# Neural-operator tower on one core: batch statistics taken in the mix, inverse and next forward transform in one stage

## Chip, core and metric

One Trainium2 chip, one core, all in fp32. The metric is the device time of one execution in microseconds (us); the kernel before has a median of 4404.04 us over three runs.

## What is computed

The part that matters is a Fourier neural operator tower of four layers over 64 images of 64x64 pixels with 64 channels:

```python
h = x @ fc0_w + fc0_b                                  # 3 -> 64 channels
for l in range(4):
    xf = rfft2(h)                                      # 32 x 16 modes are kept (16 low, 16 high rows; 16 columns)
    sc = irfft2(einsum('bixy,ioxy->boxy', xf[modes], w[l]))    # complex weights for each mode
    y = sc + einsum('bihw,oi->bohw', h, pw_w[l]) + pw_b[l]     # spectral part + pointwise part
    y = (y - mean(y)) * rsqrt(var(y) + eps) * gamma + beta     # over batch and pixels, for each channel
    h = gelu(y)
out = gelu(h @ fc1_w + fc1_b) @ fc2_w + fc2_b          # head
```

Behind it comes a tail (attention and two mixtures of experts on 64 tokens of 64 numbers for each image), which the change leaves as it is but for the places of two buffers.

## The kernel before

Data lies in pairs: a tile of 128 partitions holds two images of 64 channels (2 MB for a pair, `NP` = 32 pairs, `NG` = 8 groups of `Q` = 4 pairs). All five engines run programs written out by hand, with semaphores; each stage ends in `phase_end`, where every engine waits for the others. SP (SyncE) issues most DMAs in the order of its program, and a wait in it holds back all that follow.

- **Spectrum 0** computes the modes of the input directly from the three-channel x and stores them to `spec_in` (four stores of 4 MB, `sync_spectrum0`).
- **Mix** (`tensor_mix`) goes over 8 slabs `c` of 64 modes. A slab's weights (2 MB) and spectra (2 MB) are loaded, `rotate` on ScalarE and VectorE makes the second copy of the spectra for complex products, TensorE does 64x64 products for each mode on four tiles at once (L444, half slab v in banks 4v to 4v+3), VectorE turns the result (L480), SP stores it to `spec_out`.
- **Inverse** goes over pairs: `rows` (L579) is the inverse transform over rows, four VectorE transposes (L695) turn its result, then for each of four chunks T of 2x512 pixels `spectral` (L602) and `pointwise` (L593) add into the same PSUM banks, ScalarE copies them out with the bias (L659), VectorE takes bn_stats (L703), and ScalarE's queue stores y to `y_dram`. In layers 1 to 3 the pointwise part needs h, so the y of the layer before is loaded and passed through gelu again (L651). At the end come the statistics: `scale` and `shift`.
- **Forward** goes over pairs: load y, gelu (L843), four pixel turns (L848), `w_dft` (L803), two turns (L853), `h_dft` (L820), two turns (L862), store to `spec_in`.
- **Head**: load y, gelu (L947), `first` (L919) into three pairs of banks, gelu (L954), `second` (L930) which gathers one output row for each step.

The order of stages is spectrum 0, mix 0, inverse 0, then (forward, mix, inverse) for layers 1 to 3, the head, the tail.

Of the kernel before, what the change touches and what calls it, by code (L numbers as in the profile page):

```python
# [13 lines left out]
P = 128  # L14
# [13 lines left out]
ENGINES = 5  # L28


def dft_constants():
# [36 lines left out]
    dc[0, 0] = dc[0, K1] = 1  # L68
    consts = {"c_fw_q": fw_q, "c_gh_q": gh_q, "c_ga": np.tile(ga, (2, 1)), "c_fb2": fb2, "c_g0": g0.reshape(P, 4 * K1),
              "c_f0": f0p.reshape(97, 4, P), "c_dc": dc, "c_ident": np.eye(P),  # L70
              "c_half": np.kron(np.full((2, 2), 0.5), np.eye(C))}
    return {k: np.ascontiguousarray(v, dtype=np.float32) for k, v in consts.items()}


def tower_layout(x, fc0_w, fc0_b, w1r, w1i, w2r, w2i, pw_w):
# [12 lines left out]
    out["w_modes"] = np.stack([r, i], 2).reshape(L, NCH, P, MC, C)  # L88
    out["pw_t"] = np.ascontiguousarray(pw_w.transpose(0, 2, 1))
# [13 lines left out]
def build(nc, d, B, out):  # L103
# [5 lines left out]
    with ExitStack() as ctx:  # L109
# [8 lines left out]
        y_dram = nc.dram_tensor("y_dram", [NP, P, PX], F32, kind="Internal").ap()  # L118

# [7 lines left out]
        pw = sb("pw", [P, P])  # L127
        wst = sb("wst", [P, C])
        pwb = sb("pwb", [P, 1])
        gamma = sb("gamma", [P, 1])  # L130
# [6 lines left out]
        stats = sb("stats", [P, NP * 48])  # L137
# [4 lines left out]
        ARENA = 45800  # L142
# [36 lines left out]
        const_loaded, basis_loaded, cols_loaded = sem("const_loaded"), sem("basis_loaded"), sem("cols_loaded")  # L179
        X0_LOADS = [(0, 1), (1, 2), (2, 4), (4, 6), (6, 8)]  # L180
        x0_loaded = [sem(f"x0_loaded{i}") for i in range(len(X0_LOADS))]
        x0_load_of = [j for j, (a, b) in enumerate(X0_LOADS) for i in range(a, b)]
# [4 lines left out]
        pw0_done, pw0_copied = sem("pw0_done"), sem("pw0_copied")  # L187
# [12 lines left out]
        spec0 = [at(S0 + t * NCH * MB * MC, NCH, MB, 2, K1) for t in range(3)]  # L200
        ROUND_AT = {(i, h): (i - 3) * 2 + h for i in range(3, NQ + 1) for h in range(2)}
# [3 lines left out]
        def sync_spectrum0(sp):  # L205
            sp.dma_start(g0, d["c_g0"]).then_inc(basis_loaded, 16)
            for j, (a, b) in enumerate(X0_LOADS):
                sp.dma_start(x0_all[:, 4 * a:4 * b], d["x_rows"][4 * a:4 * b].rearrange("q p x -> p q x")).then_inc(x0_loaded[j], 16)
            for c in range(2):
                load_weights(sp, 0, c)  # L210
# [7 lines left out]
        def tensor_spectrum0(pe):  # L218

            def rows0(i):  # L220
                pe.wait_ge(x0_loaded[x0_load_of[i]], 16)
# [36 lines left out]
            pe.wait_ge(basis_loaded, 16)  # L258
# [18 lines left out]
            pe.matmul(bank[1][:, 0:1], pw[:], fc0b[:], start=True, stop=True).then_inc(pw0_done, 1)  # L277

        def vector_spectrum0(dve):
# [30 lines left out]
            dve.wait_ge(pw0_done, 1)  # L310
            for u in range(2):
                half_p = slice(u * C, (u + 1) * C)
                dve.tensor_copy(wst[half_p, :], bank[0][half_p, u * C:(u + 1) * C]).then_inc(pw0_copied, 1)
# [56 lines left out]
        def third(l, c):  # L370

            return l * (USES[c % 3] * 16) + (c // 3 * 16 + 16)

# [1718 lines left out]
```

## Time and profile before

| | |
|---|---|
| runs | 4381.96, 4404.04, 4449.41 us; median 4404.04 |
| span of the profiled execution | 4441.0 us (its own run time is not listed; the span is 8 us under the slowest run) |
| mean granted TensorE clock | 0.868 |
| PE / PEld / DVE / ACT busy | 74% / 47% / 54% / 47% |
| moved to and from HBM | 708.56 MB read, 405.14 MB written |

PE is TensorE, PEld its weight loads, DVE VectorE, ACT ScalarE, POOL GpSimd, SP SyncE; "SPq" is the queue of DMAs that SP issues. The granted clock is given as a share of 2.4 GHz. Each fp32 matmul of the program appears as two instructions. A busy share is an average over stages with different limits, so what counts is the table by stage, and inside a stage the order of the instructions.

### The profile page before, as it was taken

How to read it: one execution, taken by the hardware profiler on the slowest of the kernel's cores; microseconds unless marked ns; L12 is line 12 of the kernel's file. 1: busy time of each engine (PE TensorE's matmuls, PEld its weight loads, DVE VectorE, ACT ScalarE, POOL GpSimd, SP SyncE). 2: the span in 40 equal slices, each digit the busy share in tenths (PEclk: the TensorE clock that was granted, in tenths of full speed). 3: DMA queues.
4: the chain of work that ended last, by engine and by line, in shares of the span. 5: the costliest groups of instructions: out<-in, count | busy, mean ns of one | idle time of the engine just before them, and what ended most of it. 6: DMA issues, size and time to landing. Idle time of an engine off the chain costs nothing. (4 is left out here: it accounts for less than half of the span.)

```text
span 4441.0 us, 122046 instructions
## 1 busy us (share of the span) xinstructions
PE 3288.5 (74%) x54724; PEld 2081.7 (47%) x54724; DVE 2394.9 (54%) x3232; ACT 2086.9 (47%) x1724; POOL 28.9 (1%) x48
## 2 busy tenths in 40 slices
PE   6878866666888565596886556768877998559777
PEld 4756644455555343473554334745542222543432
DVE  3466668753666587544665777346651000554556
ACT  2133354421666644214665543236667998222321
POOL 0000000000000000000000000000000000100000
PEclk8989988888999888898998778989998999669688
DMA  8978887678999867598999676889996542003053
GB/s 305 351 192 241 238 265 271 256 288 336 345 391 380 295 249 264 228 327 330 381 377 333 248 264 249 321 294 399 391 340 231 190 173 99 10 10 68 1 97 67
DMA packets 181646, 1120.67 MB, mean 252 GB/s; under 512 B 25497, under 2 KB 31841, under 8 KB 107262
## 3 DMA queue, kind: packets, MB, share of 16 engines
q1 hardware_dynamic: 140924, 843.27, 52.7%
q10 hardware_dynamic: 39234, 269.45, 17.5%
q8 instruction: 379, 6.21, 0.5%
q0 software_dynamic: 1024, 1.05, 0.1%
q14 instruction: 85, 0.70, 0.0%
HBM read 708.56 MB, written 405.14 MB: 251 GB/s over the span
## 5 line engine op out<-in xcount | busy, mean ns | idle before, releaser
L602 PEld LDWEIGHTS bank<-fb,arena 64*64 64x64 f32 x16384 | 671.9, 199 | 512.9 <-issue 498.8
L602 PE MATMUL bank<-fb,arena 64*64 64x128 f32 x16384 | 677.9, 293 | 236.8 <-ACT arena L659 183.2
L659 ACT ACTIVATE arena<-bank,pwb 128x1024 f32<-128x1024 f32 x512 | 558.7, 1111 | 472.5 <-PE bank L593 337.0
L703 DVE BATCH_NORM_STATS2 stats<-arena 128x6 f32<-128x512 f32 x1024 | 627.8, 676 | 176.4 <-ACT arena L659 175.9
L843 ACT ACTIVATE arena<-arena,shift,scale 128x1024 f32<-128x1024 f32 x384 | 443.5, 1229 | 438.4 <-DMA arena<-y_dram 437.9
L593 PE MATMUL bank<-arena,wst 64*64 64x512 f32 x4096 | 629.9, 633 | 11.0 <-issue 10.9
L695 DVE STREAM_TRANSPOSE arena<-bank 128x512 f32<-128x512 f32 x512 | 321.1, 685 | 501.5 <-PE bank L579 501.5
L803 PE MATMUL bank<-arena,fwq 32*32 32x512 f32 x6144 | 322.6, 824 | 362.4 <-DVE arena L848 319.3
L651 ACT ACTIVATE arena<-arena,shift,scale 128x2048 f32<-128x2048 f32 x192 | 401.4, 2092 | 353.4 <-issue 206.2
L444 PE MATMUL bank<-arena 64*64 64x128 f32 x8192 | 455.4, 393 | 108.0 <-ACT arena L459 89.0
L444 PEld LDWEIGHTS bank<-arena 64*64 64x64 f32 x8192 | 395.0, 153 | 168.1 <-issue 118.8
L848 DVE STREAM_TRANSPOSE arena<-arena 128x1024 f32<-128x1024 f32 x384 | 440.1, 1203 | 16.2 <-ACT arena L843 16.2
L820 PE MATMUL bank<-arena,ghq 32*32 32x256 f32 x12288 | 366.0, 429 | 49.6 <-issue 45.1
L579 PE MATMUL bank<-arena,ga 64*64 64x512 f32 x2048 | 307.7, 619 | 127.8 <-DMA arena<-spec_out 108.5
L820 PEld LDWEIGHTS bank<-arena,ghq 32*32 32x32 f32 x12288 | 281.7, 111 | 140.5 <-issue 109.1
L803 PEld LDWEIGHTS bank<-arena,fwq 32*32 32x32 f32 x6144 | 101.0, 117 | 496.6 <-issue 486.0
L459 ACT ACTIVATE arena<-arena 64x4096 f32<-64x4096 f32 x32 | 115.9, 3621 | 448.2 <-DMA arena<-spec_in 448.2
L480 DVE STREAM_TRANSPOSE arena<-bank 128x512 f32<-128x512 f32 x256 | 159.5, 683 | 253.3 <-PE bank L444 134.8
L919 PE MATMUL bank<-arena,fc 64*128 64x512 f32 x1024 | 265.3, 626 | 17.9 <-ACT arena L947 16.5
L954 ACT ACTIVATE arena<-bank,fc1b 128x1024 f32<-128x1024 f32 x256 | 267.8, 1122 | 14.3 <-PE bank L919 14.3
L853 DVE STREAM_TRANSPOSE arena<-bank 128x1024 f32<-128x1024 f32 x192 | 227.2, 1221 | 84.9 <-PE bank L803 84.4
L579 PEld LDWEIGHTS bank<-arena,ga 64*64 64x64 f32 x2048 | 115.4, 138 | 249.9 <-issue 236.5
(195 smaller groups left out, 2364.4 us busy)
## 6 DMA issues: line engine op xcount, KB each, us to landing
arena<-y_dram SPq DMA_DIRECT2D x224, 2048.0 KB, 10.2
y_dram<-arena ACTq DMA_DIRECT2D x256, 1024.0 KB, 13.2
arena<-in_w_modes SPq DMA_DIRECT2D x32, 2048.0 KB, 17.2
arena<-spec_in SPq DMA_DIRECT2D x32, 2048.0 KB, 14.7
spec_out<-arena SPq DMA_DIRECT2D x128, 512.0 KB, 15.6
arena<-spec_out SPq DMA_DIRECT2D x112, 512.0 KB, 16.9
spec_in<-arena SPq DMA_DIRECT2D x24, 2048.0 KB, 13.6
spec_in<-arena SPq DMA_DIRECT2D x4, 4096.0 KB, 12.0
```

What stands on the lines that cost most here:

```text
L444: mm = pe.matmul(bank[4 * v + q][ROW[half], k * 2 * B:(k + 1) * 2 * B], w_sb[u][ROW[row], mode, :], s_sb[u][ROW[row], :, :, mode], start=( ...
L579: mm = pe.matmul(bank[2 * v + r][CHAN[par], :], ga[k_p, r * S:(r + 1) * S], grp[p // Q % 2][k_p, :, par * Q + q, :], start=True, stop=True ...
L593: mm = pe.matmul(bank[4 + T % 2 * 2 + i][CHAN[v], :], wst[CHAN[i], :], hin[p % 3][CHAN[i], px:px + BK], start=False, stop=True, tile_posit ...
L602: mm = pe.matmul(hpx(bank[4 + T % 2 * 2 + i][CHAN[v], :])[:, :, j * S:(j + 1) * S], a2[p % 2][CHAN[i], v, :, 4 * T + j], hpx(fb2[CHAN[i], :]),
L651: act.activation(x, x, ACT.Gelu, bias=shift[:], scale=scale[:]).then_inc(h_ready, 1)
L659: act.activation(hpx(yout[u])[:, :, T * BK:(T + 1) * BK], banks[:, 4 + T % 2 * 2:6 + T % 2 * 2, :], ACT.Identity, bias=pwb[:]).then_inc(y_ ...
L695: dve.transpose(a2[p % 2][:, :, v * HB + c0:v * HB + c0 + 16, :].rearrange("p v c r -> p c v r"), banks[:, 2 * v:2 * v + 2, :].rearrange(" ...
L703: dve.bn_stats(stats[:, p * 48 + 6 * t:p * 48 + 6 * t + 6], hpx(yout[p % 2])[:, i, T * BK:(T + 1) * BK]).then_inc(y_seen, 1)
L803: mm = pe.matmul(bank[g][QUAD[c], :], fwq[QUAD[g], s * 32:(s + 1) * 32], hT[q % 2][QUAD[g], s, :, c * CQ:(c + 1) * CQ], start=(s == 0), st ...
L820: mm = pe.matmul(bank[4 + c][QUAD[j], 0:256], ghq[QUAD[c], col:col + K1], t1[q % 2][QUAD[c], v:4:2, hh, :, ri * M2:(ri + 1) * M2], start=( ...
L843: act.activation(x, x, ACT.Gelu, bias=shift[:], scale=scale[:]).then_inc(f_ready, 1)
L848: dve.transpose(hT[p % 2][:, :, 16 * v:16 * v + 16, :].rearrange("p s h c -> p h s c"), hf[p % Q][:, v * 2 * BK:(v + 1) * 2 * BK].rearrang ...
```

## The change

1. The mean and variance of y are computed in the mix from its spectra (Parseval) and from the pointwise product, before the inverse. For this the mix gets, for each half slab, a `product` on TensorE (pointwise weights times the spectra), a ScalarE copy of it, two ScalarE squares with a sum, two VectorE cross products with a sum. The sums of squares of the pointwise part come from the stage before.
2. Since scale and shift are known ahead, one stage (`*_fuse`) does inverse, gelu, the next layer's pointwise product and the forward transform for each pair. What goes to `y_dram` is the next pointwise product p, and VectorE adds it to the spectral part one layer later.
3. The last inverse and the head are one stage (`*_last`).
4. For modes of column 0 the weights are made symmetric: GpSimd does that (`gpsimd_even`), for layer 0 in spectrum 0, for the others in fused stage 0. For layer 0 the sum of squares of the pointwise part comes from a Gram matrix of x.

The stages are now spectrum 0, mix 0, fused 0, (mix, fused) for layers 1 and 2, mix 3, last, tail. The core of the diff:

```diff
 def sync_spectrum0(sp):
...
+            load_modes(sp, 0, 0)
+            load_weights(sp, 0, 1)
+            sp.wait_ge(even_stored, 64)
+            load_even(sp, 0)
             for t in range(NB):
                 sp.wait_ge(fc0_first, 4 * t + 4)
...
+        def tensor_mix(pe, l):
+            def product(n):
+                c, v = n // 2, n % 2
...
+                if n > 1:
+                    pe.wait_ge(mixed_turned, (l * NU + n - 1) * 2)
...
+            def spectra(n):
...
+                pe.wait_ge(prod_copied, l * NU + n + 1)
...
+            product(0)
+            for n in range(NU):
+                spectra(n)
+                if n + 1 < NU:
+                    product(n + 1)
...
+            def copy_product(n):
+                v = n % 2
+                act.wait_ge(prod_done, l * NU + n + 1)
+                act.activation(x2[v], banks[:, 4 * v:4 * v + 4, :].rearrange("p q x -> p (q x)"), ACT.Copy, scale=2.0).then_inc(prod_copied, 1)
...
+        ROWS_SLOT = (0, 1)
+        Y_SLOT = (0, 0, 1, 0)
+        NEXT_SLOT = (0, 1, 1, 1)
...
+            # TensorE, y_of(p, T)
+                if T == 2 and p > 0:
+                    pe.wait_ge(squared, n * 4)
+                if T == 3:
+                    pe.wait_ge(squared, n * 4 + 1)
...
+            # TensorE, iteration n
+                if now:
+                    y_of(n, 0)
+                if before:
+                    next_of(n - 1, 2)
+                if now:
+                    y_of(n, 1)
+                if before:
+                    next_of(n - 1, 3)
+                if after:
+                    rows_of(n + 1, 0)
+                if before:
+                    w_dft(n - 1, 0)
+                if now:
+                    y_of(n, 2)
+                    next_of(n, 0)
+                if after:
+                    rows_of(n + 1, 1)
+                if before:
+                    w_dft(n - 1, 1)
+                if now:
+                    y_of(n, 3)
+                    next_of(n, 1)
+                if before:
+                    h_dft(n - 1)
...
+            def evict(p, T):
+                n = l * NP + p
+                act.wait_ge(px_turned, n * 4 + T + 1)
+                act.wait_ge(next_done, n * 4 + T + 1)
+                act.sem_inc(waited[act.engine], 1)
+                act.activation(chunk(p, T), slot(NEXT_SLOT[T]), ACT.Copy).then_inc(evicted, 1)
+                act.activation(slot(NEXT_SLOT[T]), slot(NEXT_SLOT[T]), ACT.Square, accum_out=acc[:, p * 4 + T:p * 4 + T + 1]).then_inc(squared, 1)
```

(The two comment lines in the diff name the engine; they are not in the code.) The order of the other two engines in iteration n of a fused stage: VectorE `add(n,0)`, `px_turn(n-1,2)`, `h_turn(n-2)`, `add(n,1)`, `px_turn(n-1,3)`, `turn_rows(n+1,0)`, `add(n,2)`, `w_turn(n-1,0)`, `px_turn(n,0)`, `turn_rows(n+1,1)`, `add(n,3)`, `w_turn(n-1,1)`, `px_turn(n,1)`; ScalarE `evict(n-1,1)`, `gelu(n,0)`, `evict(n-1,2)`, `gelu(n,1)`, `evict(n-1,3)`, `gelu(n,2)`, `evict(n,0)`, `gelu(n,3)`. Fused stage 0 has no adds; there `y_of` also multiplies x by its weights `wx`, and gelu reads PSUM. In `rows` the output of a matmul goes to PSUM in the order "p (c r k) -> p r k c", where it was in one piece before. In the last stage `rows` and y use slot 0 (banks 0 and 1) alone, and `first` has two slots where it had three.

## Rows read from the trace of the kernel before

**Rows 1.** Busy time by stage: window, length, busy us of each engine, clock, DMA
```profile
0.00:83.00 83.00, 51.44 (x324) 34.89 (x324) 32.71 (x35) 17.55 (x17) 0.59 (x7) 0.93 0.82 304
229.00:619.00 390.00, 314.82 (x5636) 236.96 (x5636) 251.02 (x403) 143.09 (x131) 0.00 (x0) 0.92 0.84 231
619.00:943.00 324.00, 198.60 (x6144) 128.48 (x6144) 259.59 (x256) 149.07 (x129) 0.00 (x0) 0.83 0.71 267
943.00:1097.00 154.00, 112.97 (x2048) 97.23 (x2048) 58.11 (x72) 29.08 (x9) 0.00 (x0) 0.85 0.87 327
1097.00:1521.00 424.00, 329.58 (x5636) 219.63 (x5636) 245.91 (x400) 268.12 (x195) 0.00 (x0) 0.89 0.94 354
2943.00:3362.00 419.00, 322.44 (x5636) 214.32 (x5636) 245.19 (x400) 268.00 (x194) 0.00 (x0) 0.91 0.93 358
3362.00:3774.00 412.00, 386.23 (x2048) 107.86 (x2048) 6.28 (x10) 389.25 (x321) 15.53 (x32) 0.98 0.46 165
```

**Rows 2.** Timeline of mix 1, TensorE's matmuls and VectorE's turns: start, us
```profile
954.85 55.54 PE L444 MATMUL bank<-arena 64*64 64x128 f32 x1012 [20.59 <-ACT arena L459]
...
962.16 2.51 DVE L480 STREAM_TRANSPOSE arena<-bank 128x512 f32<-128x512 f32 x4 [3.98 <-PE bank L444]
969.16 2.51 DVE L480 STREAM_TRANSPOSE arena<-bank 128x512 f32<-128x512 f32 x4 [4.49 <-PE bank L444]
```

**Rows 3.** Timeline of SP's queue, last stores of mix 1
```profile
1074.72 1.74 SPq L391 DMA_DIRECT2D spec_out<-arena  x4
```

**Rows 4.** Timeline of inverse 0 at full clock
```profile
239.38 2.44 DVE L695 STREAM_TRANSPOSE arena<-bank 128x512 f32<-128x512 f32 x4
...
241.96 1.99 PE L579 MATMUL bank<-arena,ga 64*64 64x512 f32 x8 [8.65 <-DVE arena L695]
...
245.95 1.10 PE L602 MATMUL bank<-fb,arena 64*64 64x128 f32 x32
...
246.86 1.04 PE L593 MATMUL bank<-arena,wst 64*64 64x512 f32 x8
...
247.72 1.04 PE L579 MATMUL bank<-arena,ga 64*64 64x512 f32 x8
...
247.97 1.11 ACT L659 ACTIVATE arena<-bank,pwb 128x1024 f32<-128x1024 f32 x1 [0.22 <-PE bank L593]
```

**Rows 5.** Timeline of the last `h_dft` of forward 0
```profile
931.51 2.75 PE L820 MATMUL bank<-arena,ghq 32*32 32x256 f32 x128 [1.50 <-DVE arena L862]
934.29 1.31 DVE L862 STREAM_TRANSPOSE arena<-bank 128x512 f32<-128x512 f32 x2 [2.93 <-PE bank L820]
```

**Rows 6.** Groups by line and shape: count, busy us, mean ns, idle before
```profile
L843 ACT ACTIVATE arena<-arena,shift,scale 128x1024 f32<-128x1024 f32 x384 | 443.5, 1229 | 438.4 <-DMA arena<-y_dram 437.9
L345 ACT ACTIVATE arena<-bank 128x1024 f32<-128x1024 f32 x16 | 16.3, 1023 | 31.4 <-PE bank L252 31.3
L680 ACT ACT_TABLE_LOAD x4 | 5.1, 1283 | 59.5 <-DMA y_dram<-arena 59.5
...
L848 DVE STREAM_TRANSPOSE arena<-arena 128x1024 f32<-128x1024 f32 x384 | 440.1, 1203 | 16.2 <-ACT arena L843 16.2
L1383 DVE TENSOR_TENSOR arena<-bank,arena 128x512 f32<-128x512 f32 x16 | 10.3, 688 | 11.0 <-PE bank L1247 11.0
```

**Rows 7.** Timeline of the head, TensorE alone
```profile
3606.90 1.99 PE L919 MATMUL bank<-arena,fc 64*128 64x512 f32 x8
3608.81 1.07 PE L930 MATMUL bank<-arena 128*32 128x512 f32 x8
3609.81 1.99 PE L919 MATMUL bank<-arena,fc 64*128 64x512 f32 x8
```

**Rows 8.** Spectrum 0's stores, small loads, GpSimd arithmetic: timeline, DMA, group
```profile
37.77 29.84 SPq L214 DMA_DIRECT2D spec_in<-arena  x4
...
arena<-spec_out SPq DMA_DIRECT2D x4, 256.0 KB, 3.2
...
L1570 POOL TENSOR_SCALAR arena<-arena 128x384 f32<-128x384 f32 x1 | 1.2, 1246 | 4.9 <-POOLq L171 4.9
```

More of the change, by code:

```diff
@@ L452, in scalar_mix @@
[L452 to L459 removed]
+                sp.wait_ge(mixed_stored[u], l * (NCH * 32) + NCH * 32)
+                sp.sem_inc(waited[sp.engine], 1)
@@ new lines, in turn @@
+            def turn(n):
+                c, v = n // 2, n % 2
+                if v == 0 and c > 1:
+                    dve.wait_ge(mixed_stored[c % 2], l * (NCH * 32) + (c // 2 * 64))
+                    dve.sem_inc(waited[dve.engine], 1)
+                modes = banks[:, 4 * v:4 * v + 4, :].rearrange("p q (k r b) -> p b r (q k)", k=4, r=2)
+                for j in range(2):
+                    dve.transpose(m_sb[c % 2][:, 4 * j:4 * j + 4, v, :], modes[:, 32 * j:32 * j + 32]).then_inc(mixed_turned, 1)
@@ new lines, in vector_mix @@
+            rotate(0)
+            for n in range(NU):
+                cross(n)
+                turn(n)
+                if n % 2 == 0 and n // 2 + 1 < NCH:
+                    rotate(n // 2 + 1)
+            base = l * BN_STEPS
+            dve.wait_ge(layer_loaded, l * 96 + 96)
+            dve.wait_ge(crossed, (l * NU + NU) * 2)
+            dve.sem_inc(waited[dve.engine], 1)
+            dve.tensor_tensor(acc_p[:], acc[:], acc_w[:], ALU.mult).then_inc(bn_step, 1)
+            dve.scalar_tensor_tensor(out=bn[:, 9:10], in0=dc[:, 1:2], scalar=0.5, in1=dc[:, 0:1], op0=ALU.mult, op1=ALU.add).then_inc(bn_step, 1)
@@ L845, in vector_forward @@
[L845 to L854 removed]
+            rows_of(0, 0)
@@ new lines, in tensor_fuse @@
+            rows_of(0, 1)
+            for n in range(NP + 1):
+                now, before, after = n < NP, n > 0, n + 1 < NP
+                if now:
[22 more added lines that the diff above has]
+                    h_dft(n - 1)
@@ L884, in build, with gpsimd_fuse @@
+        def gpsimd_fuse(pool, l, first):
+            pool.wait_ge(pw_loaded, l * 32 + 32)
+            pool.sem_inc(waited[pool.engine], 1)
+            gpsimd_negate(pool, l + 1)
+            if first:
+                pool.wait_ge(negated, 2)
+                for k in range(1, L):
+                    gpsimd_even(pool, k)
+                pool.wait_ge(even_stored, 16 * N_EVEN * L)
+        fc1_done, fc1_gelu, fc2_used = sem("fc1_done"), sem("fc1_gelu"), sem("fc2_used")
         fc2_ready, tok_ready = sem("fc2_ready"), sem("tok_ready")
@@ L909, in tensor_head @@
[L909 to L919 removed]
+        FC_SLOT = (2, 1)
```

1195 lines of the change are left out of this document (704 added, 491 removed).

## Prediction

> **What bounds the kernel now.** I read the table by stage first [rows 1]: its windows are cut where the first DMA of each stage is issued. The thirteen stages of the tower take 3774 us, the tail the other 667, which the change leaves alone. From 619 to 3362 run three identical layers (forward, mix, inverse), 2743 us or 914 each. The three kinds have different limits. An inverse stage of a later layer moves 354 GB/s with its DMA engines 94% busy: each pair is read and written (4 MB), and TensorE, at 329 of 424 us, is not far behind. A forward stage is short of everything: it waits for its loads, and its clock falls to 0.83. A mix stage has TensorE busy without a break once it has begun: 1012 matmuls stand in one row of 55.54 us, and VectorE's turns come each 7.00 us (962.16, 969.16) for a half slab of 128 instructions, so 54.9 ns each [rows 2]. The head is ScalarE's: 389 of 412 us [rows 1]. So bytes matter in the inverse stages (390, 424 and 419 us in the rows), and engine time or engine order in the rest.
>
> **What the change removes.** Five passes of 67 MB over `y_dram`: three reads of forward, the last inverse's write, the head's read. It removes bn_stats, and the statistics at the end of each inverse. What is late next is the question: in the fused stage each pair moves 4.5 to 5 MB, under 14 us at 354 GB/s, and I find below that the engines need far more than that. So the bytes are worth only what they held up.
>
> **Mix.** Each half slab now has a `product` on TensorE, ahead of it a wait for nothing new, and behind it a ScalarE copy (`prod_copied`) for which the next `spectra` on TensorE waits. So the product and the copy stand on TensorE's path. The product's moving operand has `b` innermost, 64 floats apart, as `spectra` has. In L444 a 128-column instruction on one of four tiles took 54.9x4 = 220 ns [rows 2]; 512 contiguous columns (L593, 8 instructions on 4 tiles in 0.86 us, 246.86 to 247.72) took 430 ns, half as much per column [rows 4]. The product gives each tile 2048 pass-columns: 3.5 us at the first rate, 1.7 at the second; I take 3.5, since its stride is that of L444. ScalarE's two squares (1024 elements, about 1.1 each by L345 [rows 6]) lie beside the product; then the copy of 2048 elements, 1.9 us (twice L345's 1.02 less one start). With 0.25 us from TensorE to ScalarE (247.72 to 247.97 [rows 4]) and 0.15 back to TensorE (VectorE's end 241.82 to 241.96 [rows 4]), a half slab takes 7.0+3.5+0.25+1.9+0.15 = 12.8 us against 7.0. VectorE's cross products, turns and rotation (6 us a half slab) and the slab's 6.3 MB in 25.7 us stay under it. The stage: 12 us to the first operand as now, 5.8 for the first product and copy, 15x12.8+7.0 = 199, 6 for the last squares, cross and turns, 22 from the last store to the next stage as now (1074.72 to 1097 [rows 1, 3]), 2 for slips: 247 against 154. Mix 0 the same +93 on its 146: 239. The bound from below is a product at 1.7 us: 11.7 a half slab, -72 us over four stages; from above, one more slow stretch of clock, +40.
>
> **Spectrum 0.** Stores of spectra now stand in SP's queue behind `wait_ge(even_stored, 64)` and `load_even`. Today they are issued from 37.77 to 67.6 and the stage ends at 83 [rows 8]. GpSimd must first do four chunks, one after another: two loads, two tensor_scalar and one tensor_tensor of 512 elements, one store. At L1570's 1.25 us for 384 elements the arithmetic is some 5 us, and a load and a store of 256 KB, at 3.2 us to landing plus their issue and waits, some 8 [rows 8]: 13 a chunk, begun at about 33 when x is in: 85. Then 16.8 MB at 350 GB/s: 48 us, 132 in all. The Gram matmuls hide in that, and the negated weights, for which the first product waits, are GpSimd's last step there. The same chunks for layers 1 to 3 (12x13 = 156 us) lie in fused stage 0, where SP asks for them only at pair 30. Bounds 90 and 150.
>
> **Fused stages, layers 1 and 2.** Engine work of one pair: VectorE 2 row turns, 4 adds, 4 pixel turns, 2 W turns at 1.2 us (L848; L1383's 0.69 for 512 elements gives the same for the add) and 1.3 of H turns: 15.7. TensorE 4 groups of y and 4 of next at 0.9, 2 of rows at 0.87, W and H DFT at 2.75 (each now 128 instructions; H took 931.51 to 934.29 [rows 5]): 14.5. ScalarE 4 gelus of 1.23 and 4 copies with squares of 2.15: 13.5 [rows 4 to 6]. No engine is near 20, but the order is written out, and banks are few: `next` and y share slots. I walk one pair from `add(n,0)` = 0. px_turn 2, h_turn, add 1, px_turn 3 end at 6.1. `evict(n-1,3)` must wait for that turn, 2.15 us; y_of(n,2) waits for its square, 0.15+0.9+0.25: add(n,2) starts at 9.65. Add, W turn, pixel turn 0 end at 13.2; evict(n,0) and y_of(n,3) again 3.5: add(n,3) at 16.7. Add and W turn end at 19.05; h_dft (0.15+2.75) must precede y_of(n+1,0) on TensorE (0.9+0.25): the next add at 23.1. That is 63% of TensorE, the share of forward, whose clock was 0.83; the gaps here are 2 to 3 us and not 7, inverse has 0.89 [rows 1]. At half clock the same walk gives some 31.5. With 0.86 in between, 24.8. A stage: 32x24.8, 6 to fill, 12 for the last pair's DFTs and 12 for its spectra to land: 824, against 914-154 = 760 now. Bounds 22 (full clock, copies at L345's 1.02 with overlap) and 26.5 a pair. SP now issues the stores too, and load(n+2) stands behind store(n-1), but two pairs ahead: over 40 us for one landing, so nothing.
>
> **Fused stage 0.** No adds; y carries L593's product (1.76 a group), and gelu reads PSUM. The same walk: gelu 0 ends at 1.2, evict 2 at 3.4, gelu 1 at 4.6, evict 3 at 6.8, y2 and gelu 2 at 10.2, evict 0 at 12.35, y3 14.3, next 1 at 15.1, h_dft 17.9, y0 19.9. TensorE is 90% busy, so 21 with the clock: 32x21+30 = 702. Now 390+324 = 714. Bounds 18.9 and 23.
>
> **Last stage.** TensorE a pair: 8 x 0.96 (`first`, 1.91 for two), 4 x 1.0 (`second`) [rows 7], 5.2 for rows and y: 16.9. ScalarE 4x1.23+8x1.05 = 13.3. Slot 0's six turns of 2.5 us are covered by them, but `first` waits for the gelu of two before, behind gelu(n,3): one stall of 1.1 us: 18.3. 32x18.3+25 = 611, against 419+412 = 831. Bounds 17.0 and 20.
>
> **Sum.** 132+239+702+247+824+247+824+247+611+667 = 4740 against the span of 4441: +299. That span lies 8 us below the slowest of the three runs, 0.8% above their median; the difference is carried over: 4404+299 = 4703.
>
> **Rivals.** (A) The waits that I walked are covered, and the busiest engine sets the pair: 16.3 us in fused 1 and 2 (VectorE) and 17.9 in fused 0 (TensorE): 552+552+603 in place of 824+824+702, -643, so 4060. For it: each engine has idle time. Against it: evict(n-1,3), evict(n,0) and h_dft each stand between two uses of a bank pair that the code names. It decides where the mean fused pair falls under 20.4 us, 3.1 below my 23.5: there the kernel is no slower than before. (B) `rows` now writes PSUM with 32 floats between columns; if that costs as the stride of L444 does, 0.9 becomes 1.75 for each half. The last stage takes all of it, +56, fused 0 about +28, fused 1 and 2 +13 each: 4813. No row shows a strided PSUM write. (C) Product, squares and copy vanish under something in the mix, which stays at 154: 4331. Against: TensorE's unbroken row. (D) Each Square between gelus reloads ScalarE's table, 1.28 us twice (the load of L680 [rows 6]): 8x1.28x96 pairs = 983 us more on a path that has no room: about 5690. Against: gelu and Identity alternate without one.
>
> The Trainium skill bears on two of these. Its page "SBUF — State Buffer", in "Door 1: The DMA port swizzle", has lines of 16 bytes in SBUF and 8 in PSUM, and says "any non-contiguous PSUM access pattern significantly slows down matmuls". Of SBUF the trace agrees (220 against 107 ns for 128 columns); of PSUM this rule is rival B, and nothing here shows it; the time by it is B's. The Trainium skill's page "ScalarE: Activation LUTs", in "Table sets: the hidden batching unit", has cheap functions such as copy and identity in every set, but does not list square beside gelu there: that is rival D.
>
> **Chances.** My forecast 0.63, A 0.12, B 0.15, C 0.07, D 0.03. The bounds, taken together and not all at one end, put my own case within 4500 to 4880. Two per cent, about what a measurement of this kernel can tell from no change, is 4316 to 4492. Faster: 0.12, all of A. Same: C and the low end of mine, 0.13. Slower: 0.75. The range 4370 to 4900 leaves out A, D, half of C and the tails.
>
> **What would show it.** VectorE's turns in mix 12.8 us apart and ScalarE's 2048-element copy ahead of each restart of TensorE; a fused pair (distance of H turns) of 23 to 25 us with VectorE about 65% busy, adds of chunk 2 and 3 waiting for matmuls that wait for a square; a first-stage end near 132 set by GpSimd; the last stage near 610 with TensorE over 90%. I am wrong if a fused pair is under 20.4 us, or the mix is under 200.

## The result and the profile after

The changed kernel takes 5179.12 us (median of four runs, 5155.51 to 5191.25) against 4415.83 on the same chip: a ratio of 1.176, 95% interval 1.169 to 1.184. It is slower, as forecast, but by 763 us where the forecast had 299. The profiled execution spans 5169.4 us at a mean clock of 0.85.

Busy time by stage of the changed kernel, with the columns of [rows 1] (window, length, busy us of PE, PEld, DVE, ACT, POOL, clock, DMA share, GB/s). The windows are spectrum 0, mix 0, fused 0, fused 1, fused 2, last:

```profile
0.00:124.20 124.20, 68.61 (x460) 50.34 (x460) 34.03 (x42) 17.58 (x17) 25.30 (x37) 0.82 0.63 230
124.20:357.80 233.60, 171.76 (x2434) 127.30 (x2434) 96.79 (x119) 97.60 (x93) 0.00 (x0) 0.80 0.61 208
357.80:1217.40 859.60, 684.66 (x15360) 368.38 (x15360) 346.36 (x320) 405.18 (x513) 71.42 (x73) 0.93 0.53 139
...
1451.90:2431.00 979.10, 652.18 (x14336) 369.08 (x14336) 488.25 (x448) 422.40 (x513) 0.37 (x1) 0.81 0.59 174
...
2666.10:3614.80 948.70, 646.38 (x14336) 366.33 (x14336) 488.46 (x448) 422.47 (x513) 0.37 (x1) 0.83 0.61 179
...
3848.40:4505.90 657.50, 606.67 (x7168) 266.20 (x7168) 242.44 (x202) 418.70 (x385) 63.40 (x128) 0.97 0.35 127
```

Beside the forecast's terms:

| stage | forecast | measured | difference |
|---|---|---|---|
| spectrum 0 | 132 | 124.2 | -8 |
| four mixes | 239+3x247 = 980 | 233.6+234.5+235.1+233.6 = 937 | -43 |
| fused 0, 1, 2 | 702+824+824 = 2350 | 859.6+979.1+948.7 = 2787 | +437 |
| last | 611 | 657.5 | +47 |
| tail | 667 | 663.5 | -4 |
| span | 4740 | 5169.4 | +429 |

So the miss lies in the fused stages (the other terms, -8, -43, +47 and -4, cancel by luck), and the question of the experiments is what stands there. Against the kernel before, by stage: the mixes take 329 us more, spectrum 0 41 more, and fused and last stages together 3445 us where inverse, forward and head took 3083 [rows 1, with the four mixes at 146 + 3x154], 362 more; the forecast had them 122 less. A half slab of the mix, which answers to [rows 2], in the timeline (start, us):

```profile
1296.98 1.88 ACT L631 ACTIVATE arena<-bank 128x2048 f32<-128x2048 f32 x1 [0.87 <-PE bank L581]
...
1299.00 7.17 PE L603 MATMUL bank<-arena 64*64 64x128 f32 x128 [2.09 <-ACT arena L631]
...
1308.59 1.06 PE L581 MATMUL bank<-arena,wneg 64*64 64x256 f32 x4
...
1309.70 1.88 ACT L631 ACTIVATE arena<-bank 128x2048 f32<-128x2048 f32 x1 [0.73 <-PE bank L581]
...
1311.72 7.25 PE L603 MATMUL bank<-arena 64*64 64x128 f32 x128 [2.07 <-ACT arena L631]
```

From one start of L603 to the next is 12.72 us: 6.98 of spectra, 3.67 of product, 0.05 to the copy, the copy's 1.88, 0.14 back. That is the sum of the prediction (12.8), where 3.5 for the product and 0.25 to the copy erred in opposite directions.

A stretch of fused 1, TensorE alone, then SyncE's queue in the same stretch:

```profile
1838.81 1.68 PE L799 MATMUL bank<-arena,ga 64*64 64x256 f32 x16
1840.41 1.49 PE L947 MATMUL bank<-arena,fwq 32*32 32x256 f32 x64
1841.84 1.17 PE L809 MATMUL bank<-fb,arena 64*64 64x128 f32 x26
1845.51 0.49 PE L809 MATMUL bank<-fb,arena 64*64 64x128 f32 x5 [2.50 <-issue]
...
1851.92 1.19 PE L809 MATMUL bank<-fb,arena 64*64 64x128 f32 x30 [0.63 <-ACT bank L1014]
1858.24 0.58 PE L809 MATMUL bank<-fb,arena 64*64 64x128 f32 x2 [5.13 <-issue]
1858.56 1.99 PE L933 MATMUL bank<-arena,wst 64*64 64x512 f32 x8
1861.39 4.55 PE L964 MATMUL bank<-arena,ghq 32*32 32x256 f32 x128 [0.84 <-DVE arena L1053]
...
1840.31 1.63 SPq L840 DMA_DIRECT2D y_dram<-arena  x2
1842.05 2.58 SPq L779 DMA_DIRECT2D arena<-y_dram  x1
```

This is the thing to see. A group of y is 32 instructions without a wait in it, but TensorE stops after 26 of them for 2.50 us, and in another group after 30 for 5.13 us, and the releaser is "issue": nothing that the profile shows. The H transform that follows (1861.39) stands in a stretch of granted clock 0.5 and takes 4.55 us against 2.75 in [rows 5]. The DMA view of 1836 to 1868, share of the DMA engines in tenths and GB/s in slices of 0.8 us:

```profile
DMA  0799999997899989989988999979731000000000
GB/s 0 300 384 387 384 394 379 374 348 154 184 266 225 174 266 266 225 174 215 328 246 287 328 328 348 430 312 369 287 141 51 8 0 20 0 0 0 20 0 0
```

By the records of single packets, 2 MB go to `spec_in` in packets of 2 KB up to 1842.4, at 374 to 394 GB/s; then the two stores to `y_dram` in packets of 8 KB, which start up to 1851.9, with the DMA engines as busy but at 154 to 266 GB/s for the most part; then the load, in packets of 16 KB, most of them started by 1858. Queue 8 carries TensorE's instructions; the page has it as:

```profile
q8 instruction: 517, 8.47, 0.7%
```

517 packets of 16 KB. TensorE has 64,580 matmuls, as many weight loads and 2848 other records, 132,008 in all: 255 a packet, so 256 slots of 64 bytes. e1 and e6 below have 119,720 and 119,653 records and 469 packets, again 255. The kernel before has 379 packets for 112,504 records: 297 a packet. Its inverse stages have 250 to 260 a packet, but its forward stages, which run as a loop on TensorE (`pe.Fori(1, NG)`, seven rounds), 390 to 594, with no packet started for up to 107 us. The fused stages have no such loop inside: the 29,424 records of fused 1 are 116 packets. So the change also put straight code in the place of looped code.

**Where TensorE stalls.** I numbered TensorE's records from the first of each stage and took every pause over 0.5 us between two weight loads with no semaphore wait between them. In fused 1 there are 108; 52 of them, 137.5 us, fall on numbers whose remainder by 256 is 76, 77 or 78. The two above are numbers 11,852 and 12,109. In fused 2 it is the same remainder, 47 pauses and 121.8 us; in fused 0, 182 to 184, 47 pauses and 116.8 us. The rest are spread over all remainders, 69 us in fused 0 and 87 to 90 in the other two, there mostly the 2.1 us ahead of L933 once a pair, a wait that the walk contains. The second piece of evidence is the time at which queue 8's packets start. One started at 1843.10 and one at 1855.88, with 12.8 us between them, and TensorE went on at 1845.51 and 1858.24: 2.4 us after each. Of the 146 pauses of the three stages 136 are like that: work resumes 2.1 to 2.6 us after a block's packet starts. Of the 196 other pauses 15 are. So these are waits for the next block of instructions, and the block is late because its packet starts late, among some 20 us of bulk packets. Together 376 us. In the last stage, which stores nothing to `y_dram`, the same count gives 6 us. In the kernel before it gives 46 us in inverse 0 and 8 to 15 in the later ones (a looped forward stage can't be numbered like that).

### The profile page after: what moved, and what is told of

Its sections match the earlier page's. It is cut to its first block and busy times, and to the rows that moved or that the text cites. A ratio compares the mean times of both kernels' runs of the same rounds, so it can differ in the third digit from the quotient of the medians.

```text
span 5169.4 us, 141776 instructions
## 1 busy us (share of the span) xinstructions
PE 3833.6 (74%) x64580; PEld 2200.9 (43%) x64580; DVE 2339.6 (45%) x2458; ACT 2245.7 (43%) x2564; POOL 173.6 (3%) x249
## 5 line engine op out<-in xcount | busy, mean ns | idle before, releaser
L826 DVE TENSOR_TENSOR arena<-bank,arena 128x1024 f32<-128x1024 f32 x384 | 468.2, 1219 | 1047.0 <-PE bank L809 1047.0
L809 PEld LDWEIGHTS bank<-fb,arena 64*64 64x64 f32 x16384 | 570.4, 197 | 639.9 <-issue 584.3
L1006 ACT ACTIVATE arena<-arena,shift,scale 128x1024 f32<-128x1024 f32 x256 | 317.7, 1241 | 862.0 <-DVE arena L826 853.7
L933 PE MATMUL bank<-arena,wst 64*64 64x512 f32 x3072 | 496.0, 687 | 146.8 <-issue 146.8
L603 PE MATMUL bank<-arena 64*64 64x128 f32 x8192 | 461.6, 393 | 132.5 <-ACT arena L631 100.0
L603 PEld LDWEIGHTS bank<-arena 64*64 64x64 f32 x8192 | 408.2, 173 | 212.8 <-issue 186.8
L1013 ACT ACTIVATE arena<-bank 128x1024 f32<-128x1024 f32 x384 | 392.2, 1021 | 199.2 <-DVE arena L1046 141.8
L799 PE MATMUL bank<-arena,ga 64*64 64x256 f32 x4096 | 321.0, 430 | 126.6 <-DMA arena<-spec_out 54.9
L1014 ACT ACTIVATE bank<-bank 128x1024 f32<-128x1024 f32 x384 | 391.7, 1020 | 0.0
L947 PE MATMUL bank<-arena,fwq 32*32 32x256 f32 x12288 | 321.7, 412 | 57.1 <-issue 45.7
L684 DVE SCALAR_TENSOR_TENSOR arena<-bank,arena 128x1024 f32<-128x1024 f32 x128 | 156.3, 1225 | 411.6 <-ACT arena L642 410.9
L1003 ACT ACTIVATE arena<-bank,shift,scale 128x1024 f32<-128x1024 f32 x128 | 154.2, 1205 | 410.2 <-PE bank L913 410.2
L575 PE MATMUL bank<-arena,wst 64*64 64x512 f32 x512 | 232.8, 1033 | 84.8 <-ACT arena L626 84.8
L642 ACT ACTIVATE arena<-bank 128x1024 f32<-128x1024 f32 x128 | 131.2, 1025 | 363.6 <-PE bank L603 355.7
## 6 DMA issues: line engine op xcount, KB each, us to landing
spec_in<-arena SPq DMA_DIRECT2D x4, 4096.0 KB, 24.8
```

The costliest lines, as they stand in the source:

```text
L603: mm = pe.matmul(bank[4 * v + q][ROW[h], k * 2 * B:(k + 1) * 2 * B], w_sb[c % 3][ROW[row], mode, :], z[ROW[row], :, :, mode], start=(swap ...
L799: mm = pe.matmul(bank[2 * s + v][CHAN[par], :].rearrange("p (c r k) -> p r k c", c=16, r=2)[:, r], ga[k_p, r * S:(r + 1) * S], grp[p // Q ...
L809: mm = pe.matmul(hpx(bank[2 * s + i][CHAN[v], :])[:, :, j * S:(j + 1) * S], a2[p % 2][CHAN[i], :, v, 4 * T + j], hpx(fb2[CHAN[i], :]), sta ...
L826: dve.tensor_tensor(chunk(p, T), slot(s), chunk(p, T), ALU.add).then_inc(y_added, 1)
L933: mm = pe.matmul(bank[2 * NEXT_SLOT[T] + v][CHAN[i], :], wst[CHAN[v], :], pb[p % NS][CHAN[v], i, T * BK:(T + 1) * BK], start=True, stop=Tr ...
L947: mm = pe.matmul(bank[4 + g][QUAD[c], 0:256], fwq[QUAD[g], s * 32:(s + 1) * 32], hT[p % 2][QUAD[g], i, :, s, c * CQ:(c + 1) * CQ], start=( ...
```

## Experiments

Each run is compared with the kernel before on its chip; the intervals are +-0.004 to 0.008. Its medians beside the runs were 4416 to 4435 us, so a difference in us between two rows can be off by some 20; the ratios and the stages of the traces are not. "Stalls" are the pauses at a block's border, counted as above, in fused 0, 1, 2.

| run | us | ratio | fused 0, 1, 2 | stalls |
|---|---|---|---|---|
| the change | 5179 | 1.176 | 860, 979, 949 | 117, 138, 122 |
| e1 half the W transform | 5071 | 1.146 | 798, 943, 957 | 100, 124, 123 |
| e2 quarter stores and loads | 4795 | 1.084 | 723, 843, 837 | 17, 33, 31 |
| e3 H transform later | 5006 | 1.133 | 840, 885, 889 | 101, 150, 158 |
| e4 copy in halves | 5064 | 1.144 | 858, 974, 962; mixes 205 to 213 | 114, 128, 124 |
| e5 = e3 + e4 | 4899 | 1.110 | 835, 885, 888 | 91, 127, 136 |
| e6 W transform in one piece | 5106 | 1.155 | 809, 961, 960 | 82, 77, 81 |
| e7 quarter loads | 5135 | 1.161 | 857, 960, 958 | 113, 119, 122 |
| e8 = e5 + e6 | 4823 | 1.092 | 758, 888, 884 | 38, 110, 108 |
| e9 quarter stores | 4943 | 1.114 | 856, 858, 844 | 113, 46, 42 |
| e10 stores on ScalarE's queue | 5226 | 1.176 | 950, 948, 947 | 179, 124, 120 |
| e11 stores in two, each at once | 4897 | 1.104 | 765, 874, 868 | 50, 58, 57 |
| e12 = e8 + e10 | 4903 | 1.104 | 871, 871, 874 | 87, 104, 101 |
| e13 stores in two, together | 4977 | 1.123 | 771, 910, 905 | 56, 87, 87 |
| e14 stores in four | 4885 | 1.102 | 745, 873, 872 | 33, 55, 61 |
| e15 = e8 + e11 | 4648 | 1.047 | 738, 817, 817 | 24, 65, 65 |
| e16 = e8 + e14 | 4644 | 1.046 | 745, 809, 818 | 26, 51, 63 |
| e17 before, stores in two | 4344 | 0.982 | | 2 in inverse 0 |

**TensorE's work.** e1 does the W transform for s = 0 alone, so half of the work is left out. e6 does all of it in one 512-column piece; that piece must also wait for the H turns of the pair before, and the first W turn for the whole piece, so e6 changes the order a little as well.

```diff
-                for s in range(2):
+                for s in range(1):                     # e1
...
-                            mm = pe.matmul(bank[4 + g][QUAD[c], 0:256], ...
-                                           hT[p % 2][QUAD[g], i, :, s, c * CQ:(c + 1) * CQ],
+                            mm = pe.matmul(bank[4 + g][QUAD[c], :], ...      # e6
+                                           hT[p % 2].rearrange("p i h s c -> p (i h) s c")[QUAD[g], :, s, c * CQ:(c + 1) * CQ],
```

> The changed kernel, with half of the W DFT of each pair left out (only s = 0, so the spectra are wrong in value): 64 of a pair's 448 matmul instructions and their weight loads go. In my walk of the pair the W DFT lies beside ScalarE's copy and square, off the chain. Theory S (TensorE's instruction stream is not delivered fast enough: the gaps of 5.5 us a pair in fused 1 in which TensorE waits for nothing): the gaps shrink at least with the number of instructions, 0.8 to 1.6 us a pair, so 75 to 150 us over the 96 fused pairs: 5030 to 5105 us. Theory O (the order of the engines alone, with links longer than I walked): less than 25 us, about 5165.

> The changed kernel with the W DFT of a pair in one piece of 512 columns in place of two of 256, as the kernel before had it: 64 matmul instructions and 64 weight loads fewer for each pair, all work kept. Theory S (supply of instructions): as with half of the W DFT left out, 80 to 110 us less, about 5085; the gaps without a releaser shrink. Theory O: the W DFT was beside ScalarE's copy, so under 25 us. It could be slower if the one piece, which must now wait for the H turns of the pair before, delays y_of(n,2).

Both have half the instructions for the W transform, a seventh fewer in the stage. Fused 0 falls by 62 and 51 us, fused 1 by 36 and 18, and fused 2 rises by 8 and 12. e6's stalls in fused 1 and 2 are 40 to 60 us less, but its clock there is 0.79 where it was 0.81 and 0.83, and TensorE is about as long busy (646 us) with a seventh fewer instructions. Both totals lie near what the theory of supply expected, but the gain sits mostly in fused 0 and the stalls of e1 fell by 29 us alone, so neither run names a cause.

**The order.** e3 puts the H transform of pair n-1 behind `y_of(n + 1, 0)`, off the walk's path.

```diff
                 if now:
                     y_of(n, 0)
+                if n > 1:
+                    h_dft(n - 2)
...
-                if before:
-                    h_dft(n - 1)
```

> The changed kernel with h_dft(n-1) moved on TensorE behind y_of(n+1,0), all work kept. By the walk of the pair the link W turn, h_dft (2.9 us), y_of(n+1,0) goes, and VectorE's own order follows: 2.8 us a pair less in fused 1 and 2, 2.0 in fused 0: -240 us, about 4940. Theory S (the supply of instructions sets the pair more than the order): the gaps grow as TensorE's work gets denser, and half or less of it is seen: 5060 to 5150.

It gives 94 and 60 us in fused 1 and 2, 2.9 and 1.9 a pair: the 2.9 + 0.15 us that the walk has for that step, less a part; in fused 0 it gives 0.6 a pair, of 2.0 expected. In all 5006 us, between the two theories (4940, 5060 to 5150). The stalls of fused 1 and 2 rose to 150 and 158, so the gain is one of order: the walk had it right, and the denser pair gave some 50 us back to the stalls of these two stages.

**The traffic.** e2 stores and loads only the first quarter of each pair's columns at `y_dram`, e7 loads a quarter and stores all, e9 stores a quarter from layer 1 on and loads all.

```diff
-sp.dma_start(y_dram[p].rearrange("(v c) (i x) -> i c v x", v=2, i=2)[i], pb[p % NS][CHAN[i]])
+sp.dma_start(y_dram[p].rearrange("(v c) (i x) -> i c v x", v=2, i=2)[i][:, :, 0:BK], pb[p % NS][CHAN[i]][:, :, 0:BK])
```

> The changed kernel, where only a quarter of each pair goes to y_dram and comes back (the rest of the tile keeps old values, so the result is wrong in value). All instructions and waits of the compute engines are the same. Theory S1 (the instruction blocks are late because bulk transfers share the DMA engines): gaps of TensorE without a releaser halve, 80 us off each of fused 1 and 2 and 40 off fused 0, about 4980. Theory S2 (the delay of a block is its own, whatever the load): no change beyond 25 us. Theory O: no change either, since no load or store was on the chain.

> The changed kernel where only a quarter of each pair is loaded from y_dram, but all of it is stored (values wrong). Loading and storing at a quarter gave 385 us. If the bytes count alike, whatever their direction, about half of it, 4990 us (fused 0, which never loaded pairs, stays as it was, 860). If only the stores count (4 KB runs written by two transfers each), it stays above 5120; if only the loads, it comes near 4800.

> From layer 1 on only a quarter of each pair is stored (leaves the rest of the values in DRAM as layer 0 left them); layer 0 stores whole, and all loads are whole. Theory (the stores hold up TensorE's instruction blocks, the loads don't): fused stages 1 and 2 fall from 979 and 949 to those of the run in which both were a quarter, 843 and 837; fused stage 0 stays at 860; in all 5179 - 136 - 112 = 4930, ratio 1.115. Rival (the two only do harm together): stages 1 and 2 halfway, 900, in all 5050. Rival (the stores are innocent): 5179.

Busy time by stage, fused 0 and fused 1 of e2, then of e9:

```profile
358.54:1081.83 723.29, 635.09 (x15360) 349.71 (x15360) 346.35 (x320) 404.45 (x513) 71.43 (x73) 0.98 0.33 96
1316.52:2159.53 843.01, 586.01 (x14336) 340.67 (x14336) 488.11 (x448) 422.58 (x513) 0.37 (x1) 0.90 0.28 86
```

```profile
357.15:1213.40 856.25, 684.24 (x15360) 366.06 (x15360) 346.33 (x320) 405.52 (x513) 71.41 (x73) 0.92 0.54 140
1447.81:2305.94 858.13, 600.82 (x14336) 346.68 (x14336) 488.11 (x448) 422.41 (x513) 0.37 (x1) 0.89 0.40 140
```

e2 comes near the stages of the prediction: 723, 843, 837 against 702, 824, 824, all engine work kept. That is 384 us, nearly twice the 200 that I expected of it. TensorE's busy time falls by 66 us as well, since its clock rises from 0.81 to 0.90. e9 shows that the stores do it: fused 0, whose stores are whole, stays at 856; fused 1 and 2 fall by 121 and 105 and their stalls from 138 and 122 to 46 and 42. e7's loads change these two stages by -19 and +9. In fused 1 and 2 e7 and e9 move the same 2.5 MB of `y_dram` a pair, so it is not the sum of the bytes. Nor is it the time that packets take of the DMA engines: their share in fused 1 is 0.48 of 960 us in e7, 461 us, less than in e13 below (0.58 of 910), and e7 has the more stalls, 119 us against 87. What e7 keeps, and e2, e9, e11, e13 and e14 don't, are the 8 KB packets of the stores.

**The queue.** In e10 ScalarE issues the stores, behind `gelu(n, 2)`, on its queue as in the kernel before; e12 does so on top of three other edits.

```diff
+                    for i in range(2):
+                        act.dma_start(y_dram[n - 1].rearrange("(v c) (i x) -> i c v x", v=2, i=2)[i], pb[(n - 1) % NS][CHAN[i]])...
```

> All work kept; the stores of a fused stage are issued from ScalarE's queue behind its third gelu, as the kernel before did, and not from SyncE's in front of the next load. Theory (packets queued behind SyncE's loads are what holds TensorE's blocks, and on a queue of their own they take 309 ns again): the idle time that waits for nothing falls by half or more, stages 780, 880, 880, in all near 4930, ratio 1.115. Rival (the bytes count, on whatever queue they are): the same stages as with SyncE's stores, 860, 979, 949, plus the issue on ScalarE, which TensorE's waits for evictions pass on: 5180 to 5250.

> The four edits that kept all work: copy of the product in halves, W transform in one piece, H transform one y later, and the stores on ScalarE's queue. If the stores' queue is worth what its own run is expected to show, 250 us in all, this gives 4823 - 150 to 200 = 4620 to 4670 (less than the sum, since fewer stalls were left), ratio 1.05; if the queue doesn't matter, 4820 to 4870. Neither theory has it at or under the kernel before.

My theory that the packets suffer behind SyncE's loads fell: the total is the same to 0.1%, fused 0 even loses 90 us, with 179 us of stalls. On top of the edits the queue costs 80 us (4903 against 4823, 87 in the fused stages), more than the 4820 to 4870 that I expected at the worst. A queue of their own doesn't free the blocks.

**The cut.** e11 cuts the store of a pair in two by columns and sends each half when its blocks are evicted. e13 sends the same halves together, when all four blocks are evicted. e14 sends four quarters, each at once.

```diff
-                sp.wait_ge(evicted, (l * NP + p) * 4 + 4)
-                for i in range(2):
-                    sp.dma_start(y_dram[p]...[i], pb[p % NS][CHAN[i]]).then_inc(p_stored[p % NS], 16)
+                for T in range(0, 4, 2):
+                    sp.wait_ge(evicted, (l * NP + p) * 4 + T + 2)
+                    x = slice(T * BK, (T + 2) * BK)
+                    for i in range(2):
+                        sp.dma_start(y_dram[p]...[i][:, :, x], pb[p % NS][CHAN[i]][:, :, x]).then_inc(p_stored[p % NS], 16)
```

> All work kept; each pair's store is cut in two by columns (the first two blocks as soon as they are evicted, the other two behind them), on SyncE's queue as before: bursts of 1 MB in place of 2 MB, packets of 4 KB. Theory (a burst of large store packets stands in front of the instruction block on each of the 16 DMA engines): the stalls get shorter, stages 1 and 2 fall by 40 to 80 us each, in all 5020 to 5100. Rival (the mean share of the DMA engines counts, not the burst): 5179 within 1%.

> All work kept; each pair's store is cut in two by columns as in the run before, but both parts are issued together when all four blocks are evicted: packets of 4 KB, the same bunch in time. Packet size theory: all of the cut's gain stays, 4897 within 1%, stages near 765, 874, 868. Bunching theory: it is gone, 5180 within 1%, stages near 860, 979, 949.

> All work kept; each pair's store is cut in four, each block as soon as it is evicted, packets of 2 KB. Both theories: less than the 4897 of two parts; the quarter-traffic run (4795) is the floor of what stalls can give back, so 4800 to 4860. A rival: eight issues per pair and four waits on SyncE's queue hold the loads back, or 2 KB packets cost more of the DMA engines' time than 4 KB ones, and it comes out above 4897.

Fused 0 and fused 1 of e11, then of e13, by stage:

```profile
357.58:1122.13 764.55, 654.36 (x15360) 356.79 (x15360) 346.30 (x320) 404.99 (x513) 71.39 (x73) 0.96 0.57 156
1356.19:2229.73 873.54, 603.54 (x14336) 348.07 (x14336) 488.11 (x448) 422.39 (x513) 0.37 (x1) 0.88 0.62 195
```

```profile
358.05:1128.78 770.73, 654.40 (x15360) 355.15 (x15360) 346.35 (x320) 405.14 (x513) 71.42 (x73) 0.97 0.54 155
1363.31:2273.63 910.32, 633.78 (x14336) 363.37 (x14336) 488.69 (x448) 422.82 (x513) 0.37 (x1) 0.85 0.58 187
```

With all work and all bytes kept, the cut gives 282 us, well over what I expected (80 to 160), and stalls fall from 376 to 164 us; the other 70 go with the clock (0.81 to 0.88 in fused 1) and were not tried by themselves. Both theories of e13 were half right: 202 us stay when the halves go together, so most of it is the cut into smaller pieces itself (twice the issues, and 8 KB packets become 4 KB; no run parts the two), and the other 80 are the bunching, nearly all of them in fused 1 and 2. Four pieces are no better than two (ratios 1.102 and 1.104, intervals overlap): that expectation missed by 25 us. e14 says one thing more: with every byte stored, block by block in 2 KB packets, fused 1 takes 873 us, and e9, which stored a quarter of the bytes in packets of that size, took 858. So of e9's 121 us some 107 come back without saving a byte.

**The copy in the mix.** e4 copies the product in two halves, so that the spectra start behind the first; e5 and e8 add the edits up.

```diff
-                act.activation(x2[v], banks[:, 4 * v:4 * v + 4, :]..., ACT.Copy, scale=2.0)
+                for h in range(2):
+                    act.wait_ge(prod_done, (l * NU + n) * 2 + h + 1)
+                    act.activation(x2[v][:, 2 * BK * h:2 * BK * (h + 1)], banks[:, 4 * v + 2 * h:4 * v + 2 * h + 2, :]..., ACT.Copy, scale=2.0)
```

> The changed kernel with the mix's copy of the product in two halves, each released by its half of the product, and the spectra of banks 0 and 1 begun after the first half. By the walk of the mix a half slab goes from 12.75 to about 10.9 us: 64 half slabs, -120 us, about 5060. If something else than product and copy sets the half slab (VectorE's turns before the next product, loads), it stays within 30 us of 5179.

> Both moves together, all work kept: h_dft behind the next y_of(n+1,0), and the mix's copy in halves. They touch different stages, so the two gains measured alone (173 and 115 us) add: about 4890 us.

> h_dft moved, copy in halves, and W DFT in one piece of 512 columns, all work kept. If the three gains add: 4890 less 80 to 100, about 4800 us. If the shorter pair leaves less time between instruction blocks, the gaps take some of it back: 4850.

A mix falls from 234 to 205 to 213, and its clock rises from 0.81 to 0.92: the copy stood on TensorE's path, as the walk of the mix had it. e4 came out at 5064 (expected 5060), e5 at 4899 (4890), e8 at 4823 (4800 if all three add, 4850 if stalls take some back).

**All together.**

> Product copied in halves, W transform in one piece, H transform one y later, and stores in two parts. The three edits alone gave 4823 with 757, 888, 884 in the fused stages; the cut in two alone took 95, 106 and 81 off them, but part of those stalls are gone already: 55 to 75 off each, in all 4600 to 4660, ratio near 1.045. Rival (both removed the same stalls): 4780 to 4823.

> The same three edits with the stores in four parts: 4560 to 4640, ratio 1.03 to 1.05, if stalls are all that is left above the walk; the rival is as for the cut in four alone.

Mix 0, fused 0 and fused 1 of e15 by stage:

```profile
123.60:328.90 205.30, 172.31 (x2434) 122.88 (x2434) 96.80 (x119) 98.53 (x109) 0.00 (x0) 0.92 0.70 237
328.90:1066.76 737.86, 621.61 (x13312) 322.30 (x13312) 342.52 (x320) 407.76 (x513) 71.41 (x73) 0.97 0.58 162
1275.93:2093.40 817.47, 581.17 (x12288) 334.18 (x12288) 491.81 (x448) 419.53 (x513) 0.37 (x1) 0.87 0.67 208
```

4648 was expected at 4600 to 4660. The four parts of e16 give the same, 4644, just above the 4560 to 4640 expected. What is left above the kernel before, 214 us, is no longer in the fused stages: fused and last stages are 2372 + 657 = 3029 us against 3774 - 83 - 608 = 3083 for inverse, forward and head of before [rows 1, with the four mixes at 146 + 3x154], so -54; the mixes are 835 against 608, +227; spectrum 0 is +41. The sum of the three is +214. The price of this change is the statistics in the mix, and the four merged stages save a quarter of it.

**The cut in the kernel before.** The same cut, issued from ScalarE in the inverse stages.

```diff
-                if T == 3:
-                    act.wait_ge(y_copied, n * 4 + 6)
+                if T % 2 == 1:
+                    act.wait_ge(y_copied, n * 4 + T + 3)
+                    x = slice((T - 1) * BK, (T + 1) * BK)
                     for v in range(2):
-                        act.dma_start(y_dram[p]...[v], hpx(yout[u])[CHAN[v]])...
+                        act.dma_start(y_dram[p]...[v][:, :, x], hpx(yout[u])[CHAN[v]][:, :, x])...
```

> The kernel before, with the stores of its four inverse stages cut in two by columns, each part issued from ScalarE as soon as its blocks are out. Theory (stalls come from bunched stores meeting instruction blocks, and an inverse of before has only 44 blocks in it): its first inverse had 41 us of idle time that waits for nothing and the later ones some 6, so at most 41 + 3 x 6 = 59 us come back, ratio 0.987 to 1.0. Rival (the bunches hold up the inverse in other ways too, by loads that land late): 4434 - 150 = 4280, ratio 0.965. Other side: two more issues a pair on ScalarE, on which TensorE waits there, cost 0.1 to 0.5 us each, 64 pairs: 4445 to 4500.

4344.12 us against 4420.44, ratio 0.982 (0.978 to 0.986): faster, clear of the noise, though not clearly by 2%. So the fair comparison of e15 is with this kernel, 304 us and not 214. Inverse 0, groups of L602 and of the copies L659 (count | busy us, mean ns | idle before and releasers), kernel before, then e17:

```profile
L602 PE MATMUL bank<-fb,arena 64*64 64x128 f32 x4096 | 173.0, 285 | 41.5 <-issue 34.7 <-ACT arena L659 6.4 <-PE bank L579 0.3
L659 ACT ACTIVATE arena<-bank,pwb 128x1024 f32<-128x1024 f32 x128 | 141.6, 1114 | 270.5 <-PE bank L593 216.2 <-DMA y_dram<-arena 50.5 <-issue 3.7
```

```profile
L602 PE MATMUL bank<-fb,arena 64*64 64x128 f32 x4096 | 156.4, 278 | 5.7 <-ACT arena L659 4.0 <-issue 1.7
L659 ACT ACTIVATE arena<-bank,pwb 128x1024 f32<-128x1024 f32 x128 | 141.9, 1115 | 206.4 <-PE bank L593 178.7 <-DVE stats L704 22.2 <-issue 5.1
```

L602's 34.7 us without a releaser are gone, and so are the 50.5 us in which the copies waited for a buffer to be stored: the first layer's inverse and forward together are 68 us shorter. By the count of pauses at block borders 46 us of inverse 0 have become 2. The expectation had only the first of the two and set 59 us as the most; it was 76, and its rival (loads that land late) had 150.

## Why the prediction was off

The direction was right, and so was the walk's order of waits as far as e3 and e4 tried it. The size was not, by 429 us, and one step, the fused pair, has 437. The 5179 us lie above the range of 4370 to 4900 and belong to none of the rivals: what made them was not among the mechanisms considered.

- **The fused pair, failed.** The step is "At half clock the same walk gives some 31.5. With 0.86 in between, 24.8", and beside it "so nothing" for SP's stores. The walk gives every instruction its duration and every wait its source, but has no term for TensorE's supply of instructions: some 920 records a pair, 3.6 blocks of 16 KB, that come over the same 16 DMA engines as the stores. I asked of the stores only whether they land in time for the next load. They do, and meanwhile they hold up the instructions: 376 us of stalls in 96 pairs, 3.9 a pair. With a quarter of the `y_dram` traffic (e2) the stalls are 81 us and the three stages come to 2403, within 53 us of the forecast. Of the 384 us that e2 takes off, 295 are stalls; the other 89 go with the clock, which rose from 0.81 to 0.90 in fused 1, but that share was not tried by itself. A measured pair is 29.2 us in fused 1, 28.5 in fused 2, 25.8 in fused 0; the shortest pair of fused 1 took 22.7 (the next 24.7), beside the 23.1 that I walked at full clock. What holds a block's packet back on its DMA engine stays open.
- **The clock.** I took 0.86 for fused 1 and 2 from gaps of "2 to 3 us and not 7". Stalls of up to 6.6 us made other gaps, and the clock was 0.81 and 0.83. The 31.5 us at half clock don't follow from the walk as printed either: its TensorE terms are 3x0.9 + 2.75 = 5.45 us, which gives 28.5. That error is small and would have lowered the forecast.
- **The order of a pair, right.** Moving the H transform off the path gave 1.9 to 2.9 us a pair (e3). Rival A (the busiest engine sets the pair) is dead: VectorE is busy 488 of 979 us.
- **Mix, right within 5%.** 12.72 us for a half slab against 12.8. The stages are 937 against 980: fifteen half slabs of 12.72 and spectra of 7.0 are 198, so all else in a stage takes 36 us where I had put 48 in mix 1 to 3 (12, 5.8, 6, 22 and 2). Rival C is dead.
- **Spectrum 0, right.** GpSimd's four chunks end at 77, I had 85; the stage ends at 124.2, I had 132.
- **Last stage, too low by 47.** In the timeline of that stage:

```profile
4018.68 1.19 PE L809 MATMUL bank<-fb,arena 64*64 64x128 f32 x32
4019.80 1.06 PE L1188 MATMUL bank<-arena 128*32 128x512 f32 x8
...
4021.86 1.09 PE L799 MATMUL bank<-arena,ga 64*64 64x256 f32 x16
4022.88 1.13 PE L1176 MATMUL bank<-arena,fc 64*128 64x512 f32 x4
...
4035.96 2.04 PE L1176 MATMUL bank<-arena,fc 64*128 64x512 f32 x8 [0.52 <-ACT arena L1240]
```

  A group of y holds TensorE for 1.12 us and half of `rows` for 1.02, so 6.5 us a pair where I put 5.2 (0.91 and 0.87 of [rows 4] would have given 5.4). A pair takes 19.26 us at clock 1.00, with one wait of 0.52 for a gelu where I had 1.1; my 18.3 was itself 0.3 over its own terms (16.9 + 1.1). So 31 of the 47 us are in the pairs, and the other 16 in the fill and the end of the stage.
- **Rival B, dead.** `rows` writes PSUM with 32 floats between columns and takes 1.02 us for a half, against 0.87 in one piece; the rival needed 1.75. The Trainium skill's page "SBUF — State Buffer", in "Door 1: The DMA port swizzle", would have every non-contiguous PSUM access slow matmuls significantly: at most 0.15 us in 0.87 of it is seen here.
- **Rival D, dead.** Gelu, copy and square alternate in fused stages with one table load at the start of each stage, so square costs no reload, although the Trainium skill's page "ScalarE: Activation LUTs", in "Table sets: the hidden batching unit", doesn't list it beside gelu.

## What to carry to other kernels

TensorE's instructions come over the DMA engines while the program runs, here one packet for every 256 of straight code. Where an engine pauses with no releaser, number its instructions; if the pauses share a remainder by 256, it waits for code, and here bulk stores made the code late. Then cut the stores before the engine's work: 4 KB pieces in place of 8 KB, sent as soon as they are ready, gave 282 us in the new kernel and 76 in the old one. A walk of waits has no term for the supply of code, so look at the bulk traffic beside an engine that runs many instructions. Whether a fused stage written as a loop would have been spared was not tried. And when statistics are moved to a place where an engine has no idle time, price that first: it was 329 us in the change as made, and 227 in e15.

## What the runs showed of the hardware

- **Store packets have two levels.** Median time of a packet's own record: 8 KB to `y_dram` 631 ns in the changed kernel, on either queue (629 on ScalarE's), and 309 ns in the second inverse of the kernel before with the same pattern; 16 KB loads 611 ns in both; 4 KB pieces 305 ns (e11), 248 (e13) or 159 (e17); 2 KB 84. Those medians mix two levels a factor of two apart, 309 and some 630 ns for 8 KB, 159 and some 310 for 4 KB. In fused 1 over eight tenths of the 8 KB packets are nearer the slow one, two thirds of e11's 4 KB packets and half of e13's. So by the byte e11's pieces are hardly faster; each just holds its DMA engine for some 305 ns in place of 631. The slow level and the stalls come together in the kernel before too: inverse 0 has a median of 556 ns and 46 us of stalls, inverse 1 has 309 ns and 8 us. What sets the level stayed open, and so does what holds a block's packet back on its DMA engine.
- The Trainium skill's page "DMA: Bandwidth & Descriptors", in "Bandwidth", has the rule to batch DMAs to 1 MiB or more. For stores beside a busy TensorE the times here go the other way: issues of 1 MB, 512 KB and 256 KB gave 5179, 4897 and 4885 us, the last two with each issue sent as soon as it was ready.
- **A sum costs an instruction.** Each activation with a sum is followed by a read of the accumulator:

```profile
L1014 ACT ACTIVATION_READ_ACCUMULATOR bank<-bank 128x1 f32 x384 | 72.8, 190 | 0.0
```

  That is 0.19 us behind each of a pair's four squares, for which TensorE waits in the walk.
- **Same code, same place.** In fused 1 and fused 2, which run one loop body, the stalls fall on the same remainder, and 41 of fused 2's 47 on the same record numbers as in fused 1.
